# Forming the next tile's keys beside the transform's products, in a fused attention, filter and expert kernel

## The chip, the cores and the metric

The kernel runs on one core of one Trainium2 chip. The metric is the device time of one execution in microseconds (us). A core has TensorE (PE, matrix products; its weight loads are listed as PEld), VectorE (DVE), ScalarE (ACT), GpSimd (POOL) and SyncE (SP, here the queue that issues all DMA transfers). They work through their own instruction queues and meet at semaphores.

## The reference

64 sequences of 32 tokens with 256 features go through three blocks, each added to its input:

```python
x = x + xattn(layernorm(x), ctx, ...)   # context attention -> FiLM -> long filter -> FiLM -> FFN
x = x + attn(layernorm(x), wq, wk, wv, wo)
x = x + ffn(layernorm(x), w1, b1, w2, b2, centroids, w_route)   # 8 experts, 2 used by gate

# inside xattn
scores = einsum('bthd,bghd->bhtg', x @ Wq, ctx @ Wk) / sqrt(32)   # 4 heads, 257 context rows of 192
topv, topi = top_k(scores, 32); attn = scatter(softmax(topv)).mean(heads)
c_t = attn @ (ctx @ Wv)
x = layernorm(x) * (1 + g*scale_in(c_t)) + g*shift_in(c_t)
y = irfft(rfft(x) * Kf)                                           # the filter, over 32 tokens
y = y * (1 + g*scale_out(c_t)) + g*shift_out(c_t)
xt = x_text + y; xt = xt + gelu(layernorm(xt) @ W1 + b1) @ W2 + b2
```

The keys are never formed: the kernel folds `Wk` into the query of each head, `qk = Wk_h q_h` (192 rows for 32 tokens), and multiplies that with the context. This is the "fold" of the change.

## The kernel before

A tile is 4 sequences (128 tokens), so there are 16 tiles. The main loop runs steps n = 1 to 18. Step n works on four tiles at once: `a` = tile n (scores, top 32 of 257), `b` = tile n-1 (attention sums, FiLM, filter, first half of the FFN), `c` = tile n-2 (second half of the FFN, self attention), `dd` = tile n-3 (experts). `following` is tile n+1; in steps 1 to 14 it exists, and its query and fold are made in step n. The order on each engine is written out by hand in the `step` function of each engine's block; each engine executes strictly in that order, apart from weight loads that TensorE may start ahead.

The query (`query`, L1078 and on) is one product of `wq` with the transposed tokens `xT`, 4 instructions into 128 columns, copied by ScalarE to `qT` (L615). The fold (`keyed`, L1084 to L1097) is 12 small products, each two instructions, with 32 rows of one head each: L1091 for 128 of the 192 rows, L1096 for the other 64. ScalarE copies them in four instructions (L633) to `qk1` and `qk2`, of which there is one buffer each. The scores (L1108, L1114, and L1117 for the mask) read them, in two halves q = 0 and q = 1 of a step.

Accumulators are eight banks of 512 columns: `SS` (two, the scores), `BB` (two, B0 and B1: FiLM, filter, FFN), `PC` (two: PA for query, context attention and gate transposes; C0 for self attention), D0 and D1 (experts). Before, the query stands in PA, the fold in the first 192 columns of SS, PA and C0.

TensorE's order in a full step, from the middle of one step to the next: `w1a` (L1128, FFN in, first half), the fold, `w1b`, then in the next step `down` (L1151), `xl3` transposes, scores q = 0, routing (L1186), `prob` times `wsel` (L1193), expert products in (L1128 into D), transposes of `am`, `z` (L1211), experts again, transposes of `z` (L1218), FiLM in (L1229), gate transpose, scores q = 1 first part (L1108), the transform `fwd` (L1246), rest of the scores (L1114, L1117), experts out 0 and 1 (L1145), the inverse transform `inv` (L1256), `xT2` transposes (L1074), FiLM out (L1263), self attention in (L1269, L1271), experts out 2 and 3, `s_mm` (L1281), the query, experts out 4 to 7, `r_mm` (L1297), `hn` transposes (L1074), self attention out (L1308), and `w1a` again.

VectorE multiplies the transform with the filter in two instructions, `had` of BB (L916) and `had` of PC (L917), ahead of the maxima and `take` of the scores' second half, the first expert sums, and `take8(a, 0, 2)`, two replacements of found maxima (L809). It adds the self attention to `x2` (L962) and makes the last probabilities (L817) and their reciprocal (L821); POOL makes `wsel` of these (L572). ScalarE's exponentials of the second half (L641) need another function table than the gelus (`ACT_TABLE_LOAD`).

Of the kernel before, what the change touches and what calls it, by code (L numbers as in the profile page):

```python
# [75 lines left out]
def build(nc, d, out):  # L76
    with ExitStack() as ctx:
# [533 lines left out]
        def _(act):  # L611
# [11 lines left out]
            def query(a):  # L623

                wait(act, s["qT_mm"], a.count(1, 1))
                copy(qT[:, :], PA[:, D:D + 128], "qT_a")

            def keyed(a):

                wait(act, s["qk_mm"], a.count(1, 1))  # L630
                for dst, at, n in ((qk1, 0, BT), (qk2, 128, BT // 2)):
                    for h, banks in ((0, SS), (2, PC)):
                        ins = A(dst[:, :, h:h + 2, :].rearrange("p b h t -> p h b t"),  # L633
                                banks[:, :, at:at + T * n].rearrange("p h (b t) -> p h b t", b=n), ACT.Copy)
                ins.then_inc(s["qk_a"], 1)
# [7 lines left out]
            def step(a, b, c, dd):  # L643
# [47 lines left out]
                if following:  # L691
                    query(following)
# [12 lines left out]
                if following:  # L705
                    keyed(following)
# [14 lines left out]
            query(first)  # L721
            keyed(first)
# [12 lines left out]
            query(Tile(1))  # L735
            keyed(Tile(1))
# [6 lines left out]
        def _(dve):  # L743
# [80 lines left out]
            def step(a, b, c, dd):  # L824
# [101 lines left out]
                if a:  # L926
                    take8(a, 0, 2)
# [142 lines left out]
        def _(pe):  # L1070
# [6 lines left out]
            def query(a):  # L1077

                wait(pe, ld_xT[a.p], a.half(16, 16))
                for k in range(2):  # L1080
                    ins = MM(PA[:, D:D + 128], wq[:, k, :], xT[a.p][:, k, :], start=k == 0, stop=k == 1)
                ins.then_inc(s["qT_mm"], 1)

            def keyed(a):  # L1084

                wait(pe, s["qT_a"], a.count(1, 1))
                wait(pe, s["mr1_v"], a.count(4, 0))
                wait(pe, s["exp_a"], a.count(4, 0))
                for h, bank in enumerate((S[0], S[1], PA, C0)):
                    rows = slice(DH * h, DH * h + DH)  # L1090
                    MM(bank[:, 0:128], wk[rows, 0:128], qT[rows, :], start=True, stop=True)  # L1091
                for u in range(2):
                    for h, bank in enumerate((S[0], S[1], PA, C0)):
                        rows = slice(DH * h, DH * h + DH)
                        pairs = qT[rows, :].rearrange("p (b u t) -> p b u t", b=BT // 2, u=2)[:, :, u, :]
                        ins = MM(bank[64 * u:64 * u + 64, 128:192].rearrange("p (b t) -> p b t", b=BT // 2), wk[rows, 128:DV], pairs, start=True, stop=True)  # L1096
                ins.then_inc(s["qk_mm"], 1)  # L1097

            def scores(a, q):

                wait(pe, s["qk_a"], a.count(1, 1))
# [17 lines left out]
            def step(a, b, c, dd):  # L1119
# [86 lines left out]
                if b:  # L1206
# [5 lines left out]
                    ins.then_inc(s["z_mm"], 1)  # L1212
                if dd:
# [22 lines left out]
                if b:  # L1236
# [5 lines left out]
                    if dd:  # L1242
                        wait(pe, s["gT_a"], one(dd))
                    for k, bank in enumerate((B0[:, 0:D], B1[:, 0:D], PA[:, D:2 * D], C0[:, D:2 * D])):
                        rows = slice(T * k, T * k + T)
                        ins = MM(bank[0:NF, :], dft_x[rows, :], xf[rows, :], start=True, stop=True)  # L1246
                    ins.then_inc(s["fwd_mm"], 1)
                if a:
                    scores_end(a, 1)
                if dd:  # L1250
                    experts(range(0, 2))
                if b:

                    wait(pe, s["had_v"], one(b))
# [82 lines left out]
            query(first)  # L1337
            keyed(first)
# [23 lines left out]
            query(Tile(1))  # L1362
            pe.wait_ge(s["qkw_sb"], 1)
            keyed(Tile(1))
# [102 lines left out]
```

## Time and profile before

| | us |
|---|---|
| median of 3 runs | 606.03 (601.78 to 606.12) |
| the profiled execution | 601.4 |
| its span, first to last instruction | 599.6 |
| PE busy in the span | 551.3 (92%) |
| DVE busy | 498.0 (83%) |
| ACT busy | 293.2 (49%) |
| POOL busy | 280.6 (47%) |

The page's chain of work that ended last puts 78% of the span to PE. About 110 us go by before the steps are full. Ends of matrix products are modelled in the profile, so PE being busy is not PE at its peak: whether a stretch is full is read from the starts. A weight load shown as idle before and released by another engine shows a wait even where PE counts as busy.

### The profile page before, as it was taken

Reading aid. Unit: us, or ns where it says so; the run is one execution under the profiler, and the core shown is the slowest. Engines: PE = TensorE matmul, PEld = TensorE weight load, DVE = VectorE, ACT = ScalarE, POOL = GpSimd, SP = SyncE. Lnnn points to the kernel's source line nnn. Section 1 sums busy time; section 2 is a strip of 40 time slices with the busy share of each in tenths; the row PEclk is TensorE's granted clock in tenths of the full one; section 3 lists DMA queues with packets and bytes.
Section 4 is the critical chain, followed back from the end, with each engine's and each line's share of the span. In section 5 each row is a group of like instructions: output and inputs, shape, how many; then the busy total and the mean of one; then the engine's idle time right before and its main releaser. Section 6 shows DMA issues by size and latency. Waiting matters only on the chain.

```text
span 599.6 us, 13084 instructions
## 1 busy us (share of the span) xinstructions
PE 551.3 (92%) x4558; PEld 399.3 (67%) x4558; DVE 498.0 (83%) x1761; ACT 293.2 (49%) x768; POOL 280.6 (47%) x656
## 2 busy tenths in 40 slices
PE   3688488999999999999999999999999999989966
PEld 2344264768686777768686768686877768675845
DVE  7997876789898988989888989898988989876443
ACT  3032242464646564555646364646564555635432
POOL 6755147625445362626363535445362636262521
PEclk9998897999999999999999999999999999999998
DMA  8488103030403030210303030304030210000000
GB/s 282 65 325 338 66 2 119 2 113 2 131 2 131 1 110 22 74 60 23 109 19 113 19 113 10 123 1 131 3 129 3 83 50 10 2 10 1 10 1 17
DMA packets 17957, 42.33 MB, mean 71 GB/s; under 512 B 2770, under 2 KB 9570, under 8 KB 17380
## 3 DMA queue, kind: packets, MB, share of 16 engines
q1 hardware_dynamic: 17892, 41.51, 20.8%
q8 instruction: 36, 0.59, 0.4%
q14 instruction: 29, 0.24, 0.1%
HBM read 39.37 MB, written 2.13 MB: 69 GB/s over the span
## 4 chain that ended last, share of the span: by engine, by line
PE 78%; DVE 3%; issue 3%; ACT 2%; POOL 2%; POOLq 0%; DVEq 0%
PE BB L1128 10%; PE D L1128 9%; PE BB L1151 9%; PE D L1145 8%; PE SS L1108 4%; PE SS L1114 3%; PE PC L1269 2%; PE PC L1308 2%; PE BB L1229 2%; PE PC L1271 2%; PE BB L1230 2%; PE BB L1264 2%; PE BB L1263 2%; PE PC L1211 2%; PE BB L1246 2%
## 5 line engine op out<-in xcount | busy, mean ns | idle before, releaser
L545 POOL TENSOR_SCALAR var_in<-mv 128x1 f32<-128x1 f32 x64 | 14.0, 219 | 240.8 <-DVE mv L774 141.1
L809 DVE MATCH_REPLACE8 work<-top,work 128x257 f32<-128x257 f32 x192 | 77.4, 411 | 0.0
L1128 PE MATMUL D<-ang,e_w 128*128 128x128 f32 x512 | 71.2, 285 | 0.0
L803 DVE MAX8 top<-work 128x8 f32<-128x257 f32 x192 | 71.0, 411 | 0.0
L1128 PEld LDWEIGHTS D<-ang,e_w 128*128 128x128 f32 x512 | 63.2, 196 | 10.1 <-issue 10.1
L1128 PE MATMUL BB<-ang,w 128*128 128x128 f32 x512 | 66.4, 284 | 1.3 <-ACT ang L701 0.9
L1145 PE MATMUL D<-expw,ang 128*128 128x256 f32 x256 | 66.0, 388 | 1.2 <-ACT ang L620 0.9
L1128 PEld LDWEIGHTS BB<-ang,w 128*128 128x128 f32 x512 | 60.8, 195 | 8.4 <-ACT ang L701 7.4
L620 ACT ACTIVATE ang<-BB,cols 128x128 f32<-128x128 f32 x128 | 36.5, 367 | 46.8 <-PE BB L1128 46.8
L641 ACT ACTIVATE expo<-SS,nmax,srs 128x257 f32<-128x257 f32 x64 | 32.7, 561 | 52.7 <-DVE work L789 52.6
L1151 PE MATMUL BB<-expw,ang 128*128 128x256 f32 x256 | 57.9, 379 | 0.0
L1145 PEld LDWEIGHTS D<-expw,ang 128*128 128x128 f32 x256 | 45.7, 190 | 10.2 <-DVE ang L842 1.9
L1151 PEld LDWEIGHTS BB<-expw,ang 128*128 128x128 f32 x256 | 47.4, 190 | 5.8
L1108 PE MATMUL SS<-ctx_t,qk 128*128 128x257 f32 x128 | 36.3, 408 | 7.1 <-ACT expo L641 5.9
L842 DVE SCALAR_TENSOR_TENSOR ang<-D,gate,ang 128x256 f32<-128x256 f32 x96 | 41.7, 476 | 1.1 <-PE D L1145 1.1
L547 POOL TENSOR_TENSOR rstd<-var_in,mhalf 128x1 f32<-128x1 f32 x64 | 36.3, 567 | 5.3
L641 ACT ACT_TABLE_LOAD x28 | 35.9, 1283 | 0.5
L620 ACT ACTIVATE ang<-D,cols 128x128 f32<-128x128 f32 x128 | 35.7, 355 | 0.2
L1108 PEld LDWEIGHTS SS<-ctx_t,qk 128*128 128x128 f32 x128 | 23.6, 204 | 15.9 <-issue 13.7
L817 DVE SCALAR_TENSOR_TENSOR prob<-work,expo 128x257 f32<-128x257 f32 x64 | 32.5, 544 | 0.0
L572 POOL TENSOR_SCALAR wsel<-head,rsum_row,tm_tile 128x32 f32<-128x32 f32 x64 | 23.6, 379 | 14.4 <-issue 13.1
L782 DVE MAX8 top<-SS 128x8 f32<-128x257 f32 x64 | 24.2, 418 | 4.7 <-PE SS L1117 4.7
(258 smaller groups left out, 1230.7 us busy)
## 6 DMA issues: line engine op xcount, KB each, us to landing
ctx_n<-in_ctx_n SPq DMA_DIRECT2D x16, 768.0 KB, 4.3
ctx_t<-in_ctxT SPq DMA_DIRECT2D x16, 514.0 KB
ctx_t<-in_ctxT SPq DMA_DIRECT2D x16, 257.0 KB
xT<-in_xT SPq DMA_DIRECT2D x16, 128.0 KB, 2.5
x_all<-in_x SPq DMA_DIRECT2D x4, 512.0 KB, 8.6
out<-out_sb SPq DMA_DIRECT2D x16, 128.0 KB, 1.7
ctx_l<-in_ctx_l SPq DMA_DIRECT2D x16, 96.0 KB, 5.0
w<-in_W SPq DMA_DIRECT2D x1, 1024.0 KB
```

What stands on the lines that cost most here:

```text
L547: link(tt(rstd[k][:, 0:1], w, mhalf[:, 0:1], ALU.pow))
L620: ins = A(dst[:, k, :], bank[:, 128 * (k % 4):128 * (k % 4) + 128], ACT.Gelu, bias=bias[:, k:k + 1])
L641: A(expo[:, 2 * q + k, :], S[k][:, 0:G], ACT.Exp, bias=nmax[:, 2 * q + k:2 * q + k + 1], scale=srs[:, a.n, 2 * q + k:2 * q + k + 1]).then_ ...
L782: V.max(top[:, 2 * q + k, 0:8], S[k][:, 0:G]).then_inc(chains["top"], 1)
L803: V.max(top[:, 2 * q + k, 8 * r8:8 * r8 + 8], work[:, 2 * q + k, :]).then_inc(chains["top"], 1)
L809: V.match_replace(work[:, 2 * q + k, :], top[:, 2 * q + k, 8 * r8:8 * r8 + 8], work[:, 2 * q + k, :], TAKEN).then_inc(chains["taken"], 1)
L817: V.scalar_tensor_tensor(prob[:, 2 * q + k, :], work[:, 2 * q + k, :], TAKEN, expo[:, 2 * q + k, :], ALU.is_equal, ALU.mult, accum_out=psu ...
L842: V.scalar_tensor_tensor(acc[k % 2][:, :], bank, gate[:, k:k + 1], acc[k % 2][:, :], ALU.mult, ALU.add).then_inc(s["acc_v"], 1)
L1108: MM(S[u][:, 0:G], qk1[:, 2 * q + u, :, :].rearrange("p h t -> p (h t)"), ctx_t1[a.p][:, 2 * q + u, :], start=True, stop=False)
L1128: ins = MM(bank[:, 128 * m:128 * m + 128], w[:, k, at:at + 128], xs[:, 128 * k:128 * k + 128], start=k == 0, stop=k == 1)
L1145: MM(bank, act2[:, k, :], e_w2[:, k, :], start=True, stop=True).then_inc(s["eo_mm"], 1)
L1151: ins = MM(B1[:, 0:D], act1[:, k, :], w2[:, k, :], start=k == 0, stop=k == HID // 128 - 1)
```

## The change

The query of the following tile is made behind the `z` products, ahead of the FiLM product, into columns 256 to 383 of B1 instead of PA; ScalarE copies it ahead of the expert gelus. The fold follows directly behind the transform `fwd`; its heads 0 and 1 go into columns 256 and up of the BB banks, heads 2 and 3 into PA and C0 as before. ScalarE copies the PC half first and then the BB half, after all scores of tile `a` are done. VectorE and ScalarE take turns at these banks: `had` of BB waits for the fold's products, the copies of BB wait for `had` of BB, and `had` of PC waits for the copies of PC. `inv` waits for all of them. `take8(a, 0, 2)` moves ahead of `had`. In the setup, tiles 0 and 1 keep the old banks.

```diff
             def keyed(a, low=BB, first=D):                       # ScalarE
                 wait(act, s["qk_mm"], a.count(1, 1))
+                wait(act, s["sc_mm"], a.count(4, 0))
+                for h, banks, shift in ((2, PC, 0), (0, low, first)):
+                    if banks is BB:
+                        wait(act, s["had_v"], a.count(2, -3))
+                    for dst, at, n in ((qk1, 0, BT), (qk2, 128, BT // 2)):
                         ins = A(dst[...], banks[:, :, shift + at:...], ACT.Copy)
+                    ins.then_inc(s["qk_a"], 1)
@@ ScalarE step
                     A(zT2[0:64, :], PA[0:64, 384:512], ACT.Copy).then_inc(s["zT_a"], 1)
+                if following:
+                    query(following)
                 if dd:
                     gelus(act2, 0, D1, e_b1, "e1a_mm", "g2a_a", dd)
                     wait(act, s["gT_mm"], one(dd))
                     copy(gateT[0:NE, :], PA[0:NE, 0:128], "gT_a")
                     gelus(act2, 1, D0, e_b1, "e1b_mm", "g2b_a", dd)
+                if following:
+                    keyed(following)
                 if a:
                     exps(a, 1)
...
-                if following:
-                    query(following)
...
-                if following:
-                    keyed(following)
@@ VectorE step
+                if a:
+                    take8(a, 0, 2)
                 if b:
                     wait(dve, s["fwd_mm"], one(b))
+                    if following:
+                        wait(dve, s["qk_mm"], one(following))
-                    V.tensor_tensor(had[0:NF, 0:2, :], BB[0:NF, :, 0:D], kern_two, ALU.mult)
+                    V.tensor_tensor(had[0:NF, 0:2, :], BB[0:NF, :, 0:D], kern_two, ALU.mult).then_inc(s["had_v"], 1)
+                    if following:
+                        wait(dve, s["qk_a"], following.count(2, 1))
                     V.tensor_tensor(had[0:NF, 2:4, :], PC[0:NF, :, D:2 * D], kern_two, ALU.mult).then_inc(s["had_v"], 1)
...
-                if a:
-                    take8(a, 0, 2)
@@ TensorE step
                     ins.then_inc(s["z_mm"], 1)
+                if following:
+                    if c:
+                        wait(pe, s["xt2_v"], one(c))
+                    if a.n == 1:
+                        pe.wait_ge(s["kt_sb"], 1)
+                    query(following)
...
                     if dd:
                         wait(pe, s["gT_a"], one(dd))
+                    if following:
+                        wait(pe, s["qT_a"], one(following))
                     for k, bank in enumerate((B0[:, 0:D], B1[:, 0:D], PA[:, D:2 * D], C0[:, D:2 * D])):
...
                     ins.then_inc(s["fwd_mm"], 1)
+                if following:
+                    if c:
+                        wait(pe, s["x2_v"], c.count(1, 0))
+                    keyed(following)
                 if a:
                     scores_end(a, 1)
                 if dd:
                     experts(range(0, 2))
                 if b:
-                    wait(pe, s["had_v"], one(b))
+                    wait(pe, s["had_v"], b.count(2, 2))
+                    if following:
+                        wait(pe, s["qk_a"], following.count(2, 2))
...
-                if following:
-                    if dd:
-                        wait(pe, s["gT_a"], one(dd))
-                    query(following)
...
-                if following:
-                    if c:
-                        wait(pe, s["x2_v"], one(c))
-                    keyed(following)
```

## Rows read from the trace of the kernel before

**Rows 1.** Windows of one step: us, busy by engine, granted clock, DMA.

```profile
300.63:332.66 32.03, 32.00 (x273) 23.77 (x273) 28.72 (x105) 17.78 (x47) 15.30 (x37) 1.00 0.19 62
```

**Rows 2.** Timeline of PE, `s_mm` to `hn`: start us, us, engine line op.

```profile
327.62 0.35 PE L1281 MATMUL PC<-ang 128*32 128x32 f32 x16
327.90 0.71 PE L1081 MATMUL PC<-xT,head 128*128 128x128 f32 x4
...
331.39 0.38 PE L1074 MATMUL BB<-head,ang 128*128 128x128 f32 x2
```

**Rows 3.** Timeline of PE, steps 15 and 16, without query and fold.

```profile
519.82 0.35 PE L1281 MATMUL PC<-ang 128*32 128x32 f32 x16
...
523.53 0.38 PE L1074 MATMUL BB<-head,ang 128*128 128x128 f32 x2
...
524.81 3.84 PE L1128 MATMUL BB<-ang,w 128*128 128x128 f32 x32
528.49 3.62 PE L1151 MATMUL BB<-expw,ang 128*128 128x256 f32 x16
...
535.06 0.64 PE L1193 MATMUL PC<-prob,wsel 128*32 128x257 f32 x8 [1.64 <-POOL wsel L572]
```

**Rows 4.** Timeline of all engines, full step, around `wsel`.

```profile
310.08 0.71 POOL L572 TENSOR_SCALAR wsel<-head,rsum_row,tm_tile 128x32 f32<-128x32 f32 x2 [0.66 <-issue]
...
311.27 0.64 PE L1193 MATMUL PC<-prob,wsel 128*32 128x257 f32 x8
```

**Rows 5.** Timeline of PE, full step, around the old fold.

```profile
300.63 2.05 PE L1128 MATMUL BB<-ang,w 128*128 128x128 f32 x16
302.61 0.38 PE L1091 MATMUL SS<-qT,head 32*128 32x128 f32 x2
...
303.35 2.05 PE L1128 MATMUL BB<-ang,w 128*128 128x128 f32 x16
305.24 3.62 PE L1151 MATMUL BB<-expw,ang 128*128 128x256 f32 x16
```

**Rows 6.** Timeline of all engines, full step, around `z`.

```profile
315.02 0.41 DVE L876 SCALAR_TENSOR_TENSOR z<-ctx_l,am,PC 128x192 f32<-128x192 f32 x1 [0.65 <-PE PC L1211]
...
315.84 0.27 PE L1218 MATMUL PC<-head,z 128*128 128x128 f32 x1
```

**Rows 7.** Issue of `xT` in the timeline, and the page's DMA issues.

```profile
309.84 0.43 SPq L334 DMA_DIRECT2D xT<-in_xT  x1
...
xT<-in_xT SPq DMA_DIRECT2D x16, 128.0 KB, 2.5
```

**Rows 8.** Timeline of PE, full step, from the transform on.

```profile
319.81 0.46 PE L1246 MATMUL BB<-ang,cols 32*96 32x256 f32 x2
...
321.06 0.28 PE L1117 MATMUL SS<-mask_t,ones_b 1*128 1x257 bf16 x2
...
322.33 0.64 PE L1256 MATMUL BB<-had,dft_y 96*32 96x256 f32 x8
...
324.90 1.05 PE L1269 MATMUL PC<-ang,qk_w 128*128 128x128 f32 x8
```

**Rows 9.** Timeline of ScalarE, full step, two of the fold's copies.

```profile
304.00 0.41 ACT L633 ACTIVATE qk<-PC 128x256 f32<-128x256 f32 x1
...
304.42 0.32 ACT L633 ACTIVATE qk<-PC 128x128 f32<-128x128 f32 x1
```

**Rows 10.** Timeline of VectorE and ScalarE, full step, behind the transform.

```profile
320.28 1.28 ACT L641 ACT_TABLE_LOAD   x1
...
321.17 0.68 DVE L917 TENSOR_TENSOR had<-PC,kern_f 96x512 f32<-96x512 f32 x1
...
323.15 1.02 ACT L641 ACTIVATE expo<-SS,nmax,srs 128x257 f32<-128x257 f32 x2 [1.58 <-DVE work L789]
...
324.06 0.38 ACT L615 ACTIVATE ang<-PC 128x256 f32<-128x256 f32 x1
```

More of the change, by code:

```diff
@@ L621, in gelus, with query, keyed @@
                 ins.then_inc(s[done], 1)
-            def query(a):
+            def query(a, bank=B1):
                 wait(act, s["qT_mm"], a.count(1, 1))
-                copy(qT[:, :], PA[:, D:D + 128], "qT_a")
-            def keyed(a):
+                copy(qT[:, :], bank[:, D:D + 128], "qT_a")
+            def keyed(a, low=BB, first=D):
                 wait(act, s["qk_mm"], a.count(1, 1))
-                for dst, at, n in ((qk1, 0, BT), (qk2, 128, BT // 2)):
-                    for h, banks in ((0, SS), (2, PC)):
+                wait(act, s["sc_mm"], a.count(4, 0))
[3 more added lines that the diff above has]
+                    for dst, at, n in ((qk1, 0, BT), (qk2, 128, BT // 2)):
                         ins = A(dst[:, :, h:h + 2, :].rearrange("p b h t -> p h b t"),
-                                banks[:, :, at:at + T * n].rearrange("p h (b t) -> p h b t", b=n), ACT.Copy)
-                ins.then_inc(s["qk_a"], 1)
+                                banks[:, :, shift + at:shift + at + T * n].rearrange("p h (b t) -> p h b t", b=n), ACT.Copy)
+                    ins.then_inc(s["qk_a"], 1)
             def exps(a, q):
@@ L720, in _ @@
             first = Tile(0)
-            query(first)
-            keyed(first)
+            query(first, PA)
+            keyed(first, SS, 0)
             exps(first, 0)
@@ L734, in _ @@
             A(qk_w[:, :, :].rearrange("p a b -> p (a b)"), C0[:, :], ACT.Copy, scale=0.25).then_inc(s["qkw_sb"], 1)
-            query(Tile(1))
-            keyed(Tile(1))
+            query(Tile(1), PA)
+            keyed(Tile(1), SS, 0)
             act.wait_ge(s["kt_mm"], 1)
@@ L1075, in transposes, with query, keyed @@
                 ins.then_inc(s[done], 1)
-            def query(a):
+            def query(a, bank=B1):
                 wait(pe, ld_xT[a.p], a.half(16, 16))
                 for k in range(2):
-                    ins = MM(PA[:, D:D + 128], wq[:, k, :], xT[a.p][:, k, :], start=k == 0, stop=k == 1)
+                    ins = MM(bank[:, D:D + 128], wq[:, k, :], xT[a.p][:, k, :], start=k == 0, stop=k == 1)
                 ins.then_inc(s["qT_mm"], 1)
-            def keyed(a):
+            def keyed(a, low=BB, first=D):
                 wait(pe, s["qT_a"], a.count(1, 1))
-                wait(pe, s["mr1_v"], a.count(4, 0))
-                wait(pe, s["exp_a"], a.count(4, 0))
-                for h, bank in enumerate((S[0], S[1], PA, C0)):
+                if low is SS:
+                    wait(pe, s["mr1_v"], a.count(4, 0))
+                    wait(pe, s["exp_a"], a.count(4, 0))
+                banks = (low[:, 0, first:first + DV], low[:, 1, first:first + DV], PA[:, 0:DV], C0[:, 0:DV])
+                for h, bank in enumerate(banks):
                     rows = slice(DH * h, DH * h + DH)
@@ L1092, in keyed @@
                 for u in range(2):
-                    for h, bank in enumerate((S[0], S[1], PA, C0)):
+                    for h, bank in enumerate(banks):
                         rows = slice(DH * h, DH * h + DH)
@@ L1099, in scores @@
             def scores(a, q):
-                wait(pe, s["qk_a"], a.count(1, 1))
+                wait(pe, s["qk_a"], a.count(2, 2))
                 if q == 0:
@@ L1336, in _ @@
             pe.wait_ge(s["wqc_v"], 1)
-            query(first)
-            keyed(first)
+            query(first, PA)
+            keyed(first, SS, 0)
             pe.wait_ge(s["fills"], N_FILLS)
@@ L1361, in _ @@
             ins.then_inc(s["qkw_mm"], 1)
-            query(Tile(1))
+            query(Tile(1), PA)
             pe.wait_ge(s["qkw_sb"], 1)
-            keyed(Tile(1))
+            keyed(Tile(1), SS, 0)
             pe.wait_ge(s["film_a"], 1)
```

## Prediction

> **What bounds the kernel now.** I read the busy time by stretch first, then the instructions in order of time for one step (300.63 to 332.66 us), then the last steps, which lack parts of the work. In a full step of 32.03 us TensorE is busy for 32.00 and VectorE for 28.72, at a granted clock of 1.00, which is 2.4 GHz [rows 1]. TensorE's ends are modelled, so "busy" may hide short waits, and the question for each edit is whether its stretch of the queue is really full. Two places are not. The kernel shows this itself, since its last step with a tile `a` (n = 15) has no following tile, so no query and no key fold.
>
> From the products of the context scores (`s_mm`, L1281) to the transposes of `hn` (L1074), VectorE and ScalarE have a chain to run: maximum, exponential, reciprocal, transpose, and then `hn`. With the query in between this takes 331.39 - 327.62 = 3.77 us [rows 2]. Without it, it takes 523.53 - 519.82 = 3.71 [rows 3]. The old query therefore costs only 0.06 us.
>
> From the start of `w1a` to the next `prob` by `wsel` product (L1193), VectorE runs without a pause from `x2` to `probs(b, 1)`, then POOL makes `wsel`. POOL ends at 310.08 + 0.71 = 310.79 and TensorE uses it at 311.27 [rows 4]. In the last step, where TensorE waited for POOL, the distance from `w1a` to this product was 535.06 - 524.81 = 10.25 us [rows 3]; in a full step it is 311.27 - 300.63 = 10.64. So TensorE can come at most 0.39 us earlier there, whatever is taken out ahead.
>
> **The old places.** The fold between `w1a` and `w1b` costs (305.24 - 300.63) - (528.49 - 524.81) = 4.61 - 3.68 = 0.93 us of TensorE [rows 3, 5]. Taking it out returns 0.39, because of that limit; the other 0.54 becomes a wait for `wsel`. Taking the query out returns 0.06. ScalarE's four copies there lay behind TensorE's `w1b` and return nothing: the second gelu waited for `w1b` anyway.
>
> **The query's new place.** It stands behind the `z` products. Four instructions of 128 columns, at 3.68 us for 32 of the same shape [rows 3], make 0.46 us. What could hide it is TensorE's wait for `z`: VectorE's `z` ends at 315.02 + 0.41 = 315.43, and its transpose starts at 315.84 because the expert products ahead of it last that long [rows 6]. There is no wait, so the query costs 0.46. From below I take 0, if it fell into an unseen bubble. ScalarE gets a copy of about 0.3 us there, ahead of the gelus, which have room. Its operand `xT` is issued at 309.84 and lands 2.5 us later [rows 7], at 312.3; the query would run at about 314.8. It has been needed only at 327.90 so far, so 2.5 us of cover remain out of 15.6.
>
> **The fold's new place.** Count from the transform's first product, F = 319.81 [rows 8]. The fold takes 303.35 - 302.61 = 0.74 us from its first instruction to the one after it [rows 5]. Of this I take 0.65, since the end of a 32-row group, about 0.1, was already paid by the transform. The upper bound is the 0.93 of its old slot. The lower bound is its streamed columns alone: the four row groups run side by side, and each has two instructions of 128 columns and four of 64, which at 3.68 / 32 = 0.115 us for 128 columns [rows 3] makes 4 x 0.115 = 0.46.
>
> The Trainium skill, TensorEngine Tiling (Array Packing), section Key Properties, says that a change of tiling mode drains the engine. By that rule the fold beside the 32-row transform saves a change, and 0.93 would become 0.74 or less. The rows agree in direction, but the saving is one of a few tenths, and it is inside my 0.65.
>
> **The new waits, which are what I fear.** Now `inv` (L1256) needs both halves of `had` and both halves of the copies. The second half of `had` waits for the first two copies, and these wait for all four scores of the tile, since `qk1` and `qk2` are single. The scores' last product ends at 321.06 + 0.28 = F + 1.53 [rows 8]; with the fold ahead it is F + 2.18. Two copies of 0.41 and 0.32 us, overlapping a little, take about 0.6 [rows 9] and end at F + 2.8. Then comes the second `had`, 0.68 us [rows 10], to F + 3.53, and `inv` starts at F + 3.6. Without a wait it would be at 322.33 - F + 0.65 = F + 3.17 [rows 8]. So TensorE waits 0.43. What queues behind the waiting instructions: on TensorE all that follows; on VectorE the maxima of scores 2 and 3, `take`, then ScalarE's exponentials; on ScalarE the exponentials' table load. Moving `take8(a, 0, 2)` ahead fills VectorE's pause before `had` and is otherwise free.
>
> The Trainium skill, PSUM — Partial Sum Buffer, section PSUM bank collisions raise a hardware error, says that two engines may not touch one bank in the same partitions at once, reads included. That rule speaks against the change: with the fold in the banks that `had` reads, it turns the two engines' reads into turns. No run here shows a collision. By the rule the wait above stands; without it both engines would read at once, `inv` would come at F + 3.17 and the sum would be 0.43 a step less.
>
> A second, smaller wait follows. The exponentials began 323.15 - 321.17 = 1.98 us after the second `had`, and the copy of `xT2` another 0.91 later, for 0.38 [rows 10]. The second `had` now starts at F + 2.85, so `xT2` is ready at F + 6.13. The products that read it would be due at (324.90 - F) + 0.65 + 0.43 = F + 6.17 [rows 8], but their weight load comes first, about 0.1 us. I charge 0.12. The table load of 1.28 us [rows 10] now follows the copies, from F + 3.4 to 4.7, and the exponentials are due at F + 4.84, so it is hidden by 0.15. If copies come later by more than that, it lands on the path one for one.
>
> **Sum.** Per full step: query +0.46, fold +0.65, wait for `had` +0.43, wait for `xT2` +0.12, old query -0.06, old fold -0.39, together +1.21 us. The full steps with a following tile are n = 3 to 14, so 12, which is 14.5 us. In steps 1 and 2 TensorE waits often, so the query is free, but the waits around `had` are not; for the two together I take 0.3 (bounds -1 and +2). The sum is 14.8 us. The profiled execution took 601.4 (span 599.6), so it becomes 616.2. The median of the runs, 606.03, lies 4.6 above that execution and the lowest 0.4 above, so the same loss would show as anything from 616 to 621. I say 618.5.
>
> **Rivals.**
> (A) The forecast, slower by 0.6 to 1.8 us a step (7 to 22 us): 609 to 628. It rests on rows of the same kernel without the moved work. Chance 0.67.
> (B) It doesn't show. The handover is quicker than I make it: fold 0.46, no wait for `had` or `xT2`, query 0.46, less 0.06 and 0.39 = +0.47 a step at most, or the limit of 0.39 is looser and the full 0.93 comes back: -0.07. Time 600 to 607, or up to 611 against the slower of the runs. For it: busy times that may hide slack. Against it: the chain of copies and `had` stands behind the scores by construction. Chance 0.14.
> (C) Faster. The place is the drain between the transform and the next products: if the fold's row groups run inside the transform's own end, it adds 0.1, and if `inv` finds `had` ready and the query is hidden, the step is 0.10 - 0.06 - 0.39 = -0.35, or -0.9 if the old slot returns all. That is -4 to -11 us, 590 to 602. It decides only if the distance from the transform to `inv` stays under 3.0 us. Against it is the transform's 32-row stretch, which shows no drain as long as 0.65. Chance 0.08.
> (D) Dearer. ScalarE's copies come 0.4 us or more later, the table load comes onto the path, and `xT2`, `yb` and `hn` follow: +1.8 to 2.5 us a step, 623 to 636. Chance 0.11.
>
> One per cent, about what a measurement of this kernel can tell from no change, is 6 us, or 0.5 us a step. Slower by more: A and D, 0.78. Within: B, 0.14. Faster: C, 0.08. The range 607 to 629 holds A, the upper part of B and the lower part of D.
>
> **What would show it.** In a step of the changed kernel: a period near 33.2 us where it was 32.03; `inv` 3.6 us after the transform's first product (2.52 before), with TensorE's idle there put down to `had`; the second `had` waiting for ScalarE's copies; the product with `wsel` waiting for POOL, at 10.25 us after `w1a`; the query adding 0.45 ahead of the `z` transposes. The clock should stay at 1.00, since the added waits are of half a microsecond; a fall to 1.2 GHz would make all of this dearer. I am wrong if `inv` comes within 3.2 us, or if the `wsel` product comes under 10 us after `w1a`.

## The result and the profile after

The changed kernel takes 621.53 us (median of 4 runs, 619.2 to 621.63) beside 605.14 for the kernel before (601.78 to 606.12). The ratio is 1.0278, with a 95% interval of 1.0241 to 1.0315. It is slower, by about 16 us. The profiled execution took 619.2 us with a span of 617.2, so 17.6 above the 599.6 of before.

A full step now has a period of 33.23 us, where it was 32.03 [rows 1]. Its window (us, busy time of PE, weight loads, DVE, ACT and POOL, granted clock, DMA) shows one more microsecond that TensorE doesn't fill, at an unchanged clock:

```profile
309.65:342.88 33.23, 32.20 (x274) 23.66 (x274) 28.81 (x105) 17.84 (x47) 15.50 (x37) 1.00 0.18 60
```

The same step in the timeline of PE (start us, us, engine line op out<-in, idle before and its releaser). L1137 into BB is `w1a` and `w1b`, L1160 `down`, L1202 the product with `wsel`, L1088 the query, L1263 the transform, L1100 the fold, L1279 the inverse, L1292 the first self attention products, L1304 `s_mm`, L1081 into BB the `hn` transposes:

```profile
309.65 3.84 PE L1137 MATMUL BB<-ang,w 128*128 128x128 f32 x32
313.32 3.62 PE L1160 MATMUL BB<-expw,ang 128*128 128x256 f32 x16
...
319.97 0.64 PE L1202 MATMUL PC<-prob,wsel 128*32 128x257 f32 x8 [0.54 <-POOL wsel L572]
...
323.55 0.71 PE L1088 MATMUL BB<-xT,head 128*128 128x128 f32 x4
324.09 1.06 PE L1137 MATMUL D<-ang,e_w 128*128 128x128 f32 x8
...
328.95 0.46 PE L1263 MATMUL BB<-ang,cols 32*96 32x256 f32 x2
...
329.46 0.28 PE L1100 MATMUL BB<-qT,head 32*128 32x128 f32 x2
...
330.09 0.70 PE L1123 MATMUL SS<-ctx_t,qk 64*128 64x257 f32 x4
330.72 0.28 PE L1126 MATMUL SS<-mask_t,ones_b 1*128 1x257 bf16 x2
330.94 1.13 PE L1154 MATMUL D<-expw,ang 128*128 128x256 f32 x4
332.46 0.64 PE L1279 MATMUL BB<-had,dft_y 96*32 96x256 f32 x8 [0.39 <-DVE had L926]
...
335.06 1.16 PE L1292 MATMUL PC<-ang,qk_w 128*128 128x128 f32 x8
...
337.88 0.35 PE L1304 MATMUL PC<-ang 128*32 128x32 f32 x16
...
341.60 0.38 PE L1081 MATMUL BB<-head,ang 128*128 128x128 f32 x2
...
342.88 2.39 PE L1137 MATMUL BB<-ang,w 128*128 128x128 f32 x19
```

Two new waits stand in it. The inverse waits 0.39 us for `had`, and the product with `wsel` waits 0.54 for POOL. Behind the first stands the handover, in the timeline of ScalarE and VectorE (L636 are the copies of the fold, L923 and L926 the two halves of `had`, L644 the exponentials and their table):

```profile
330.33 0.69 DVE L923 TENSOR_TENSOR had<-BB,kern_f 96x512 f32<-96x512 f32 x1 [0.32 <-PE PC L1105]
331.13 0.55 ACT L636 ACTIVATE qk<-PC 128x256 f32<-128x256 f32 x2 [1.55 <-PE SS L1126]
331.57 0.56 ACT L636 ACTIVATE qk<-BB 128x256 f32<-128x256 f32 x2
331.72 0.69 DVE L926 TENSOR_TENSOR had<-PC,kern_f 96x512 f32<-96x512 f32 x1 [0.70 <-ACT qk L636]
332.15 1.28 ACT L644 ACT_TABLE_LOAD   x1
333.71 1.02 ACT L644 ACTIVATE expo<-SS,nmax,srs 128x257 f32<-128x257 f32 x2 [0.28 <-DVE work L792]
```

ScalarE waits for the mask products of the scores (L1126), not for the fold: its copies begin 331.13 - 328.95 = 2.18 us after the transform. VectorE waits 0.70 for them, and TensorE for VectorE. The table load is hidden with 0.28 to spare.

Where the time of a step went, by distances between the first instructions of groups on TensorE (w = product with `wsel`, F = transform, inv = inverse, v = self attention products, s = `s_mm`, down = `down` of the next step), all in us:

| kernel | w to F | F to inv | inv to v | v to s | s to down | down to w | step |
|---|---|---|---|---|---|---|---|
| before | 8.54 | 2.52 | 2.57 | 2.72 | 9.65 | 6.03 | 32.03 |
| changed | 8.98 | 3.51 | 2.60 | 2.82 | 8.67 | 6.65 | 33.23 |
| difference | +0.44 | +0.99 | +0.03 | +0.10 | -0.98 | +0.62 | +1.20 |

Twelve steps of +1.20 are 14.4 of the 17.6 us. Another 1.4 had come together by the `wsel` product of step 3, and 1.6 fell in step 16, which contains no part of the fold. There TensorE waits for `wsel` and then runs slowly for some microseconds:

```profile
551.02 0.68 PE L1202 MATMUL PC<-prob,wsel 128*32 128x257 f32 x8 [1.71 <-POOL wsel L572]
551.63 2.08 PE L1137 MATMUL D<-ang,e_w 128*128 128x128 f32 x8
```

The same eight products took 1.16 in a full step. A row over two of these microseconds shows why (the last three numbers are granted clock, DMA share and GB/s):

```profile
552.00:554.00 2.00, 2.00 (x11) 2.00 (x11) 0.00 (x0) 0.13 (x1) 1.33 (x4) 0.50 0.00 0
```

A granted clock of 0.50 is the 1.2 GHz level, in one stretch, after two waits of 0.47 and 1.71 us. The kernel before had both waits (0.47, and 1.64 [rows 3]) without the slow stretch. Whether it belongs to the change is open. Among the kernels below with the same two waits (the second of 1.48 to 1.66), runs 2, 3, 4, 6 and both of 9 have the stretch in their profiled execution, run 5, which also has the fold at its new place, hasn't, and neither have runs 1 and 7 with the old one. The 1.4 us of the first steps are no safer: the profiled executions come to the `wsel` product of step 3 at anything from 119.1 to 126.6 us, with a granted clock of 0.77 from 85 to 100 us in the kernel before and 0.91 from 100 to 120 us in the changed one. What is sure is the +1.20 of a full step, at a clock of 1.00 in both.

### The profile page after: what moved, and what is told of

It reads as the page before. It is cut to its first block, busy times and chain, and to the rows that moved or that the text cites. A ratio compares the mean times of both kernels' runs of the same rounds, so it can differ in the third digit from the quotient of the medians.

```text
span 617.2 us, 13126 instructions
## 1 busy us (share of the span) xinstructions
PE 553.9 (90%) x4558; PEld 400.5 (65%) x4558; DVE 502.5 (81%) x1761; ACT 294.1 (48%) x768; POOL 283.2 (46%) x656
## 4 chain that ended last, share of the span: by engine, by line
PE 53%; DVE 17%; issue 7%; POOL 7%; ACT 3%; POOLq 0%; DVEq 0%; ACTq 0%
PE D L1137 9%; PE D L1154 4%; DVE top L806 4%; DVE ang L845 3%; PE PC L1292 3%; PE PC L1327 2%; DVE work L812 2%; PE BB L1137 2%; PE PC L1294 2%; POOL wsel L572 2%; PE SS L1117 2%; PE BB L1244 2%; PE BB L1245 2%; PE BB L1287 2%; PE BB L1286 2%
## 5 line engine op out<-in xcount | busy, mean ns | idle before, releaser
L1154 PE MATMUL D<-expw,ang 128*128 128x256 f32 x256 | 70.4, 398 | 2.0 <-ACT ang L620 0.9
L1137 PE MATMUL D<-ang,e_w 128*128 128x128 f32 x512 | 71.4, 286 | 0.0
L1137 PEld LDWEIGHTS D<-ang,e_w 128*128 128x128 f32 x512 | 64.7, 200 | 6.4 <-issue 6.4
L1137 PEld LDWEIGHTS BB<-ang,w 128*128 128x128 f32 x512 | 61.8, 201 | 7.5 <-ACT ang L706 7.4
L1137 PE MATMUL BB<-ang,w 128*128 128x128 f32 x512 | 64.5, 287 | 1.3 <-ACT ang L706 0.9
L1160 PE MATMUL BB<-expw,ang 128*128 128x256 f32 x256 | 57.9, 379 | 0.0
L1160 PEld LDWEIGHTS BB<-expw,ang 128*128 128x128 f32 x256 | 47.4, 190 | 5.8
L644 ACT ACTIVATE expo<-SS,nmax,srs 128x257 f32<-128x257 f32 x64 | 32.7, 562 | 24.9 <-DVE work L792 24.7
L572 POOL TENSOR_SCALAR wsel<-head,rsum_row,tm_tile 128x32 f32<-128x32 f32 x64 | 23.8, 382 | 14.4 <-issue 13.1
```

The lines of the kernel that those rows point to most:

```text
L572: nc.gpsimd.tensor_scalar(wsel[:, k, :], sel[:, :], rsum_row[:, k:k + 1], tm_tile[:, k:k + 1], ALU.mult, ALU.mult).then_inc(s["wsel_g"], 1)
L644: A(expo[:, 2 * q + k, :], S[k][:, 0:G], ACT.Exp, bias=nmax[:, 2 * q + k:2 * q + k + 1], scale=srs[:, a.n, 2 * q + k:2 * q + k + 1]).then_ ...
L1137: ins = MM(bank[:, 128 * m:128 * m + 128], w[:, k, at:at + 128], xs[:, 128 * k:128 * k + 128], start=k == 0, stop=k == 1)
L1154: MM(bank, act2[:, k, :], e_w2[:, k, :], start=True, stop=True).then_inc(s["eo_mm"], 1)
L1160: ins = MM(B1[:, 0:D], act1[:, k, :], w2[:, k, :], start=k == 0, stop=k == HID // 128 - 1)
```

## The experiments

The theory on trial: every term of the sum lies on TensorE's queue, so each can be taken out by itself and the terms add. The rival: only the turns between VectorE and ScalarE cost something, and the query and the old places don't matter. For each kernel the step is read from its own trace, since most of its full steps agree to about 0.05 us (single ones are up to 0.17 longer), while whole runs of one kernel scatter by up to 1.9% (run 2: 611.79 to 623.19).

**1. The query alone.** The kernel before, with the new place of the query only.

```diff
@@ kernel before, TensorE, behind the z products; ScalarE's copy behind zT
+                if following:
+                    query(following)          # into B1
@@ behind s_mm
-                if following:
-                    query(following)
```

> The kernel before with the query alone moved behind the z products; the fold stays between w1a and w1b in its old banks. Theory (each term lies on TensorE's queue): the query adds 0.44 us there and returns 0.05 at the old place, so a full step goes from 32.03 to about 32.42 us and the kernel is 4 to 5.5 us slower (ratio about 1.008). Rival (only the turns between VectorE and ScalarE cost, the query is hidden): the step stays at 32.03 and the time is that of before.

Measured: ratio 1.0107 (1.0077 to 1.0137), step 32.42. The distance from `wsel` to the transform went from 8.54 to 8.99, so the query costs 0.45; from `s` to `down` it went from 9.65 to 9.60, so its old slot was worth 0.05. The query is a third of the loss and has nothing to do with turns. The rival falls for this term. The runs lost more than the step explains (12 x 0.40 = 4.8 us, 0.8%): in the profiled one another 3.3 us had come together by step 3.

**2. The query one step earlier.** The changed kernel, with the query for the tile after the following one at the old place, and its tokens loaded a step earlier. The fold needs its `qT` only in the next step.

```diff
+                second = next_tile(following)
@@ TensorE and ScalarE, at the old place
+                if second:
+                    query(second, PA)
@@ SyncE
-                    wait(sp, s["qT_mm"], a.count(1, -1))
-                    sp.dma_start(xT[a.p][:, :, :], d["xT"][a.n])...
+                    t = next_tile(a)
+                    if t:
+                        wait(sp, s["qT_mm"], t.count(1, -1))
+                        sp.dma_start(xT[t.p][:, :, :], d["xT"][t.n])...
```

> The changed kernel with the query made one step earlier, at its old place behind the self attention's scores, for the tile after the following one (its tokens are loaded one step earlier). The fold stays beside the transform. Theory: the step loses the query's 0.44 and pays 0.05, from 33.23 to about 32.84, so 4.7 us faster than the changed kernel and a ratio of about 1.020 to before. Rival (the query was hidden at its new place): 33.2, ratio 1.028.

Measured: ratio 1.0181 (1.0119 to 1.0242), step 32.77. From `wsel` to F it is 8.54 again. The wait for `wsel` shrank by 0.07 as well.

**3. Two buffers of the copied fold.** The changed kernel; ScalarE no longer waits for the last scores of the tile before.

```diff
-        qk1 = sb("qk1", [128, BT, H, T])
+        qk1 = [sb(f"qk1_{i}", [128, BT, H, T]) for i in range(2)]      # qk2 likewise
-                wait(act, s["sc_mm"], a.count(4, 0))
+                wait(act, s["sc_mm"], a.count(4, -4))
```

> The changed kernel with two buffers for the copied fold (qk1, qk2), so ScalarE's copies need not wait for the last scores of the tile before. Theory: copies start about 1.1 us after the transform's first product where they now start 2.18 after it, the second had follows at 1.8 to 2.0, the inverse transform waits for nothing (3.04 after the transform in place of 3.51) and the wait for xT2 goes, so 0.6 us a step back: 32.63, ratio about 1.016. Rival (the turns are the whole loss): 32.0 a step, ratio 1.00. Rival (bank turns, not the scores, delay the copies): no change, 33.2.

Measured: ratio 1.0101 (1.0081 to 1.0122), step 32.57. The timeline of ScalarE, VectorE and PE, with the transform at 323.90:

```profile
325.22 0.55 ACT L636 ACTIVATE qk<-PC 128x256 f32<-128x256 f32 x2 [0.70 <-PE PC L1105]
...
325.90 0.68 DVE L926 TENSOR_TENSOR had<-PC,kern_f 96x512 f32<-96x512 f32 x1
...
326.01 0.55 ACT L636 ACTIVATE qk<-BB 128x256 f32<-128x256 f32 x2 [0.24 <-DVE had L923]
...
326.95 0.64 PE L1279 MATMUL BB<-had,dft_y 96*32 96x256 f32 x8
```

The copies begin 1.32 after the transform in place of 2.18, the second `had` follows the first without a wait, and the inverse comes at 3.05 with no wait. So 0.60 us of the step (0.46 from F to inv, 0.14 from inv to s) were the wait for the scores, passed on through ScalarE and VectorE; the rest of the 0.66 (33.23 less 32.57) came back at the product with `wsel`. The turns themselves cost nothing once the wait is away: `had` and copies still alternate here, and ScalarE's 0.24 for `had` is off TensorE's path. This is the largest single term, and the second buffer is enough to remove it. The other way round, a single buffer without the turns, was not run. An estimate from the rows of the changed kernel: the copies of BB end at 331.57 + 0.56 = F + 3.18, and the inverse writes over what they read, so it would come at about F + 3.2 in place of 3.51. The turns then carry up to 0.3 us of this wait, but only while the copies are late.

**4. The fold behind the scores.** The changed kernel, with the fold between the scores' mask product, which uses one row, and the experts' products, which use all 128, and no longer beside the transform.

```diff
                     ins.then_inc(s["fwd_mm"], 1)
-                if following:
-                    keyed(following)
                 if a:
                     scores_end(a, 1)
+                if following:
+                    keyed(following)
```

> The changed kernel with the fold behind the rest of the scores in place of directly behind the transform. Theory: the fold then costs about 0.9 us of TensorE, as in its oldest place, where it costs 0.52 beside the transform; but the copies could start nearly as early as now, so part of it is covered by the wait for had: the inverse transform at about 3.65 after the transform (3.51 now), the step 33.35 to 33.45, ratio 1.030 to 1.034. Rival (the place beside the transform saves nothing): the fold costs 0.52 there too and the step is 33.2.

Measured: ratio 1.0303 (1.0279 to 1.0327), step 33.23 to 33.3. My theory missed here. The timeline of PE, with the transform at 332.76:

```profile
334.01 0.28 PE L1126 MATMUL SS<-mask_t,ones_b 1*128 1x257 bf16 x2
334.02 0.37 PE L1100 MATMUL BB<-qT,head 32*128 32x128 f32 x1
...
334.75 1.13 PE L1154 MATMUL D<-expw,ang 128*128 128x256 f32 x4
...
336.42 0.64 PE L1279 MATMUL BB<-had,dft_y 96*32 96x256 f32 x8 [0.54 <-DVE had L926]
```

The next group, the experts' products, starts 334.75 - 332.76 = 1.99 us after the transform. In the changed kernel it is 330.94 - 328.95 = 1.99 too. The fold costs the same in both places, so the transform itself is not needed to make it cheap. But each place has a neighbour of few rows, and the fold runs beside its end: here it starts 0.01 us after the first mask product, which has 0.22 to itself in the changed kernel (330.72 to 330.94), and in the changed kernel it starts 0.51 after the transform, where the next group used to start at 0.62. Between `w1a` and `w1b` it costs 0.93 [rows 3, 5]: it starts 1.98 us after `w1a`, 0.14 more than its 16 instructions need (1.84, half of 3.68), takes 0.74, and `w1b` takes another 0.05 over 1.84. So of the 0.41 that this place costs more, 0.19 lie at its entry and exit. The other 0.22 are, in run 4, the start beside the mask products, and in the changed kernel the start beside the transform and a quicker second pair of products, 0.11 each. What it pays for is not settled: I have no run that puts the fold beside 128-row products on both sides anywhere else.

**5. Part of the fold twice.** Eight of its 24 instructions, the same values, done twice beside the transform.

```diff
+                for _ in range(2 if twice else 1):
                     for h, bank in enumerate(banks):
                         MM(bank[:, 0:128], wk[rows, 0:128], qT[rows, :], start=True, stop=True)
```

> The changed kernel with the first four of the fold's products (8 of its 24 instructions, the 128-row part) done twice, writing the same values. It measures what a group of 32-row products costs beside the transform. Theory (streamed columns): two instructions of 128 columns for each row group running side by side, about 0.22 to 0.25 us for the fold, and because copies and had follow it, the same on the step: 33.45 to 33.5. Rival (the fold fills the transform's drain and the wait for had covers it): less than 0.1.

Measured: step 33.45, ratio 1.032 (1.0281 to 1.0359). The inverse came at 3.74 in place of 3.51. So it costs 0.22 us, as much as two instructions of 128 columns in each of four row groups that run side by side. The wait for `had` covers none of it, because the copies and `had` stand behind the fold.

**6. Two maxima ahead of `x2`.** The changed kernel, with 0.75 us of VectorE's work moved out of the chain from `x2` to `wsel`, into its wait for `x2`. **7.** The same in the kernel before.

```diff
                 if a:
                     take8(a, 0, 3)
+                    find8(a, 1, 1)
                 if c:
                     wait(dve, s["o2_mm"], one(c))
...
                     probs(a, 0)
-                    top8(a, 1, 1)
+                    take8(a, 1, 1)
```

> The changed kernel with two of VectorE's maxima (0.75 us, find8 of scores 2 and 3) moved out of the chain from x2 to wsel, ahead of x2, where VectorE waits 0.76 us. Theory: the wait of 0.54 us for wsel goes, since it is what was left of the old fold's 0.93; the step goes from 33.23 to about 32.7, ratio about 1.017. Rival (the wait only moves, to another product or to x2): 33.2, ratio 1.028.

> The kernel before with the same two maxima moved. TensorE doesn't wait for wsel there. Theory: no change, 32.03 a step, ratio 0.998 to 1.002. Rival (VectorE's load as such bounds the step): faster, up to 0.5 us a step.

Measured: in the changed kernel step 33.00, ratio 1.0228 (1.0191 to 1.0266); in the kernel before 32.03 and 0.9993 (0.9967 to 1.0019), no change, as expected. In the changed kernel the theory missed: 32.7 was expected, and only 0.23 of the 0.54 came back. The timeline of POOL, VectorE and PE says why:

```profile
350.80 0.73 POOL L599 TENSOR_TENSOR ang<-ang,rows 128x256 f32<-128x256 f32 x1
351.48 0.91 POOL L604 TENSOR_TENSOR out_sb<-ang 128x256 f32<-128x256 f32 x1
...
350.86 0.95 DVE L820 SCALAR_TENSOR_TENSOR prob<-work,expo 128x257 f32<-128x257 f32 x1
...
351.74 0.94 DVE L820 SCALAR_TENSOR_TENSOR prob<-work,expo 128x257 f32<-128x257 f32 x1
...
353.91 0.64 PE L1203 MATMUL PC<-prob,wsel 128*32 128x257 f32 x8 [0.31 <-POOL wsel L572]
```

Both probabilities took about 0.94 us beside POOL's two additions. In the changed kernel the first had taken 0.52: it began when 0.23 us of the first addition were left. POOL's own queue isn't what holds `wsel` back: the additions end at 352.39, and the second probability at 352.68.

**8. POOL's additions moved.** The changed kernel, with `xt_b` right behind POOL's norm of `xt`, and the output sum one step later.

```diff
@@ POOL
+                if dd and dd.n > 0:
+                    finish(Tile(dd.n - 1))       # out_sb = acc[0] + acc[1], behind norm(1, c)
...
                     norm(0, b)
+                    nc.gpsimd.tensor_tensor(xt_b[:, :], xt[:, :], b2[:, :], ALU.add).then_inc(s["xtb_g"], 1)
```

> The changed kernel with two of POOL's 128x256 additions (the FFN bias for xt2 and the output sum) moved away from VectorE's last probabilities: the first right after POOL's norm of xt, the second one step later, behind norm 1. Moving the two maxima alone had lifted only 0.23 of the 0.54 us wait for wsel, and both last probabilities then took 0.94 us, beside these additions, where the first had taken 0.5. Theory (VectorE's products of two SBUF operands run at half speed beside POOL's additions): the second one goes from 0.94 to 0.43, the wait for wsel loses about 0.45 and the step goes from 33.23 to about 32.75, ratio about 1.018. Rival (the 0.94 has another cause, such as VectorE's own order): the step stays at 33.2.

Measured: ratio 1.1003 (1.0961 to 1.1046), step 37.4 in most steps. The expected part happened: both probabilities take 0.42, and the wait for `wsel` is gone (down to w 6.03). But from `s` to `down` it is 9.13 in place of 8.67, because the moved addition now ran beside another operation of VectorE (run 10 shows it), so that step 3, in which nothing waits for the tokens, still takes 33.08 and not the 32.75 expected. And the whole kernel takes 44 us more than the changed one, lost at another place. The timeline of SyncE's queue and of PE:

```profile
344.82 0.34 SPq L341 DMA_DIRECT2D out<-out_sb  x1
345.20 0.43 SPq L334 DMA_DIRECT2D xT<-in_xT  x1
...
347.60 0.68 PE L1092 MATMUL BB<-xT,head 128*128 128x128 f32 x4 [2.69 <-DMA xT<-in_xT]
348.12 1.46 PE L1141 MATMUL D<-ang,e_w 128*128 128x128 f32 x8
349.38 0.42 PE L1237 MATMUL PC<-head,z 128*128 128x128 f32 x1
349.59 0.42 PE L1238 MATMUL PC<-head,z 128*64 128x128 f32 x1
349.80 1.91 PE L1141 MATMUL D<-ang,e_w 128*128 128x128 f32 x8
```

The load of the tokens for the query stands in SyncE's queue behind the store of the output, and so behind POOL's sum. In the changed kernel its row is

```profile
318.86 0.43 SPq L334 DMA_DIRECT2D xT<-in_xT  x1
```

1.11 us ahead of the `wsel` product; here it is 3.94 behind it. The query used to be 15 us away from the load. At its new place the query waits for the load in 11 steps, for up to 2.7 us, and after the wait shown the eight expert products take 1.91 and not 1.06, at a granted clock of 0.50. From `wsel` to F it is 13.36 in place of 8.98. So the change took 13 us of cover from a load. That did no harm in the changed kernel, except in step 1 (0.6 us), but only 2.0 us were left there: issued at 318.86, 2.7 to landing, needed at 323.55.

**9. Edits together.** The query a step earlier and two buffers; then the maxima as well.

> The changed kernel with the query one step earlier and two buffers of the copied fold, nothing else. Theory, terms add: 33.23 less 0.39 less 0.60 = 32.24 a step, ratio about 1.006. Rival (the two share a wait): 32.5 or more.

> The changed kernel with all three: query one step earlier, two buffers, and the two maxima ahead of x2. Theory: what is left of the change is the fold at 0.52 beside the transform in place of 0.93 between w1a and w1b, so 32.03 less 0.41 = 31.62 to 31.75 a step, 3.5 to 5 us faster than before, ratio 0.992 to 0.995. Rival (TensorE meets another limit, the chain of the self attention or of z on VectorE): 32.0 or more, ratio 1.000 or above.

Measured: step 32.17 and ratio 1.0073 (1.0037 to 1.0109) for the two, step 32.01 and ratio 1.0038 (1.0001 to 1.0075) for the three. The two add up. The three missed their number by 0.3 us, which is the wait for `wsel` beside POOL's additions, as in 6.

**10. All four.** With POOL's additions moved as in 8, which is harmless once the tokens are loaded a step earlier.

> The changed kernel with the query a step earlier, two buffers of the copied fold, the two maxima ahead of x2, and POOL's two additions moved away. Theory: nothing but the fold at 0.52 in place of 0.93 is left: 31.6 to 31.7 a step, 3 to 5 us faster than before, ratio 0.992 to 0.996. Rival (what the three together reached, 32.01 a step, is a limit of another kind): 32.0, ratio 1.00.

Measured: step 32.15, ratio 1.0057 (1.0026 to 1.0088). The wait for `wsel` is gone (6.04), but `s` to `down` became 9.25 in place of 8.72. The timeline of POOL and VectorE:

```profile
337.94 0.73 POOL L604 TENSOR_TENSOR ang<-ang,rows 128x256 f32<-128x256 f32 x1
...
337.89 0.82 DVE L969 TENSOR_SCALAR pn_c<-p_c,rsum_c 128x32 f32<-128x32 f32 x1
```

This theory missed too. POOL's addition now hit the normalising of `p_c`, in the chain to `r_mm`, which takes 0.24 when alone.

**11. All four, with that addition behind `hn`.** One more wait puts it beside VectorE's replacements of maxima.

```diff
                     norm(0, b)
+                    wait(pool, s["hn_v"], b.count(1, 1))
                     nc.gpsimd.tensor_tensor(xt_b[:, :], xt[:, :], b2[:, :], ALU.add).then_inc(s["xtb_g"], 1)
```

> As the version with all four edits, but POOL's addition of the FFN bias waits for hn, so that it runs beside VectorE's replacements of maxima and not beside the normalising of p_c, which took 0.82 in place of 0.24 us there and held back r_mm and hn (4.51 us from the context products' end to the self attention's out product, 3.99 before). Theory: that 0.5 us goes, and the step is 31.62 to 31.7 in place of 32.15; with 12 full steps 4 to 5 us less than before, of which slower first steps may take some: ratio 0.991 to 0.997. Rival (the addition slows whatever runs beside it): the step stays above 32.0.

Measured: 600.51 us beside 604.46, ratio 0.9956 (0.9927 to 0.9985), step 31.63. That is faster than before by 0.4%, a small difference that rests on 11 and 16 runs. The profiled execution doesn't show it as a whole (span 600.2 beside 599.6): its full steps save 4.8 us, but it comes to the `wsel` product of step 3 at 124.6 us and not at 119.1, with a granted clock of 0.80 from 100 to 120 us, where the one before had 1.00. The timeline of VectorE, POOL and PE:

```profile
332.77 0.24 DVE L970 TENSOR_SCALAR pn_c<-p_c,rsum_c 128x32 f32<-128x32 f32 x1
...
334.77 0.73 POOL L605 TENSOR_TENSOR ang<-ang,rows 128x256 f32<-128x256 f32 x1 [1.90 <-DVE ang L977]
...
335.08 0.41 DVE L824 MATCH_REPLACE8 work<-top,work 128x257 f32<-128x257 f32 x1
...
339.96 3.62 PE L1175 MATMUL BB<-expw,ang 128*128 128x256 f32 x16
...
346.00 0.64 PE L1219 MATMUL PC<-prob,wsel 128*32 128x257 f32 x8
```

The distances of all kernels, from one step of each trace:

| kernel | w to F | F to inv | inv to v | v to s | s to down | down to w | step |
|---|---|---|---|---|---|---|---|
| 1, query alone | 8.99 | 2.52 | 2.57 | 2.71 | 9.60 | 6.03 | 32.42 |
| 2, query a step earlier | 8.54 | 3.52 | 2.59 | 2.82 | 8.73 | 6.58 | 32.78 |
| 3, two buffers | 8.98 | 3.05 | 2.57 | 2.71 | 8.67 | 6.63 | 32.61 |
| 4, fold behind scores | 8.99 | 3.66 | 2.56 | 2.77 | 8.67 | 6.64 | 33.29 |
| 5, part twice | 8.98 | 3.74 | 2.60 | 2.81 | 8.68 | 6.64 | 33.45 |
| 6, maxima ahead | 8.98 | 3.52 | 2.59 | 2.82 | 8.67 | 6.42 | 33.00 |
| 7, the same in before | 8.54 | 2.53 | 2.56 | 2.72 | 9.65 | 6.03 | 32.03 |
| 8, POOL's order | 13.36 | 3.52 | 2.60 | 2.81 | 9.13 | 6.03 | 37.45 |
| 9, two edits | 8.54 | 3.05 | 2.56 | 2.72 | 8.72 | 6.63 | 32.22 |
| 9, three edits | 8.54 | 3.05 | 2.56 | 2.72 | 8.72 | 6.42 | 32.01 |
| 10, four edits | 8.54 | 3.05 | 2.56 | 2.72 | 9.25 | 6.04 | 32.16 |
| 11, four, behind `hn` | 8.54 | 3.05 | 2.56 | 2.72 | 8.72 | 6.04 | 31.63 |

In the last row `s` to `w` is 14.76, where it was 15.68 in the kernel before. That is 0.92 less, all of what the fold had cost at its old place (0.93 [rows 3, 5]). Beside the transform it costs 0.53. The difference of 0.40 is the whole gain that the idea of the change has to give, once the query, the buffer and the chain to `wsel` no longer take it. The kernel before with POOL's additions moved alone was not run; TensorE doesn't wait for `wsel` in it, and run 7 shows that moving the maxima does nothing there.

## Why the prediction was right

The predicted 618.5 us stands beside the measured 621.53, inside the range, and the sign and most of the loss came from the step: 33.24 predicted, 33.23 measured. The sum for the profiled execution, 616.2, is 3.0 below its 619.2, nearly all of it outside the full steps. By its own steps:

| term | predicted | measured | from |
|---|---|---|---|
| query, new place | +0.46 | +0.44 | w to F; run 1 gives 0.45 |
| fold beside the transform | +0.65 | +0.52 | transform to the rest of the scores, 1.14 in place of 0.62 |
| wait for `had` | +0.43 | +0.47 | F to inv, 0.99 less 0.52 |
| wait for `xT2` | +0.12 | +0.13 | inv to v and v to s |
| query, old place | -0.06 | -0.05 | run 1, s to down |
| fold, old place | -0.39 | -0.31 | s to w: 15.68 less 0.05, to 15.32 |
| step | +1.21 | +1.20 | |

What carried it was the last step with a tile `a`, which has no query and no fold [rows 3]: it priced both old places without a model, and both prices held. The copies were forecast to start at F + 2.18, and they did, though with some luck: the fold was 0.13 shorter than forecast, and the copies came 0.13 after the listed end of the last mask product (330.72 + 0.28 = F + 2.05), where I had put no delay. That the 0.54 us left over from the fold's old place would turn into a wait for `wsel` is in the trace, and runs 6 and 11 show that it was this wait and no other: without it the full 0.92 came back.

**Mis-sized.** The fold was 0.52 and not 0.65. Of its old 0.74 I had taken off 0.1 once, and no row gave me that 0.1; the trace has two such savings. Its first product starts 0.51 after the transform's first, 0.11 ahead of where the next group used to start, while the transform still runs, and its second pair of products follows the first after 0.11 in place of 0.22. It was luck that the sum of a step came out at 1.20 all the same: the old fold returned 0.31 and not 0.39, and the wait for `had` was 0.04 longer. The first steps and step 16 were put at 0.3 us and took about 3 in the profiled execution: 1.4 up to step 3, and 1.6 from one stretch at 1.2 GHz, on which the prediction had nothing, and which run 5, with the same fold and the same waits, doesn't show.

**Not settled.** I set the saving at the transform down to the neighbourhood of two 32-row groups. Run 4 takes the transform away from the fold, and the fold costs the same, but it gives it a one-row product as its new neighbour, so it doesn't decide between this reason and another. The rule on changes of mode in the Trainium skill, TensorEngine Tiling (Array Packing), section Key Properties, which I had weighed there, is neither borne out nor refuted by that run; what makes the place between `w1a` and `w1b` 0.4 us dearer is open.

**Half right.** I named the turns at the banks as the reason for the wait. Run 3 keeps all the turns and loses the wait. The reason is the single buffer of `qk1` and `qk2`, which ties the copies to the last scores. In the prediction's chain both stand, and I priced the right one, but the sentence that without the bank rule both engines would read at once and save 0.43 says too much: without that rule the copies would still have waited for the scores, and the inverse for the copies, so by the estimate at run 3 about 0.3 us would have been saved. Rival D (the table load comes onto the path) did not occur; its cover was 0.28 us. Rivals B and C fall with the changed kernel's own step: +1.20, the inverse at 3.51, and 10.32 from `w1a` to the `wsel` product.

**Not seen.** The tokens' load was noted as hidden, with 2.5 us of cover left; it was 2.0. Run 8 shows how thin that was: one addition moved on POOL delayed it by way of SyncE's queue and cost 44 us.

## What to carry to other kernels

Price the old place of a moved piece of work by a step of the same kernel that lacks it: here the slot was worth 0.31 of the 0.93 us that the work took, because another chain ended just behind it. A piece moved from a slot with slack into a full one pays its full price, and a copy into a single buffer waits for that buffer's last reader wherever the products stand. Before a reader of a load moves ahead, look at what stands in front of the load in its queue. When the time of one engine's operation doubles, look at what its neighbour runs in the same microsecond before you look at its queue.

## What the runs showed of the hardware

VectorE's product of two SBUF operands (128x257) took 0.42 us alone and 0.94 beside POOL's 128x256 additions; its scaling of a 128x32 tile took 0.24 alone and 0.82 beside one such addition; its replacements of maxima took 0.41 beside the same addition, and 0.41 on the average of the page. I had not expected this to matter, and it set 0.38 us of a step (32.01 with three edits, 31.63 in run 11). The Trainium skill, SBUF — State Buffer, section SBUF: two separate sides, says that VectorE operations with two SBUF inputs or in a two-port mode share a port pair with GpSimd as an exclusive lock, held for the whole instruction. The traces agree in the main for the probabilities: the second one of run 6 began when 0.65 us of an addition were left, and 0.42 and 0.65 make 1.07, where 0.94 was measured. For the scaling, which has one SBUF input, the page would need a two-port mode, which no run here shows by itself, and in run 10 the scaling is listed 0.05 us ahead of the addition and was slow all the same.

In run 8 TensorE waited for the tokens in 11 steps, for up to 2.7 us. In 9 of them products behind the wait then ran at half speed, up to 1.92 us for eight that take 1.06; in the other two, behind waits of 2.60 and 2.66 us, they kept their 1.06. One stretch of the step shown there, with the granted clock third from the end:

```profile
349.60:351.00 1.40, 1.40 (x8) 1.40 (x7) 0.00 (x0) 0.94 (x4) 1.40 (x2) 0.50 0.88 354
```

So the granted clock of that execution was 0.953 in the mean, beside 0.977 in the changed kernel. The waits of about half a microsecond in the changed kernel's full steps left the clock at 1.00.

Small products of 32 rows in four row groups side by side cost 0.22 us for two more instructions of 128 columns in each group (run 5), and the whole fold 0.52 in two places and 0.93 in a third.
